# The order of GpSimd's work in an attention step: the projection's subtraction ahead of the head's centring

## The reference

```python
ln_out = _ln(hidden_states, ln_w, ln_b)
q = _fp8_linear_pertensor(ln_out, wq, wq_scale, q_in_scale).reshape(b, s, g, hpg, d)
q = _ln(q, qln_w, qln_b)
k = _fp8_linear_pertensor(ln_out, wk, wk_scale, k_in_scale).reshape(b, s, g, d)
k = _ln(k, kln_w, kln_b)
v = _fp8_linear_pertensor(ln_out, wv, wv_scale, v_in_scale).reshape(b, s, g, d)
core = _gqa(q, k, v).reshape(b, s, nh * d)
...
cat = jnp.concatenate([core, xout], axis=-1)
catq = _div_clamp_fp8(cat, proj_smooth)
return jnp.einsum('bsi,oi->bso', catq, wproj) * (proj_in_scale * proj_w_scale)
```

## Time and profile before

| | us |
|---|---|
| median of 3 runs | 1187.11 |
| lowest and highest | 1186.66, 1187.77 |
| the profiled execution: its time | 1185.83 |
| the profiled execution: its span | 1184.0 |
| TensorE busy | 894.8 (76%) |
| VectorE busy | 957.7 (81%) |
| ScalarE busy | 723.2 (61%) |
| GpSimd busy | 401.2 (34%) |

### The profile page before, as it was taken

The page is one execution under the profiler, slowest core; times in us unless marked ns, Lnnn a source line. Parts: engine busy times, 40 slices in busy tenths (PEclk is TensorE's granted clock), DMA queues, the critical chain, the costliest instruction groups (busy, mean ns, idle before and its releaser), DMA issues. The chain is left out here.

```text
span 1184.0 us, 22559 instructions
## 1 busy us (share of the span) xinstructions
PE 894.8 (76%) x6878; PEld 785.4 (66%) x6878; DVE 957.7 (81%) x2509; ACT 723.2 (61%) x2536; POOL 401.2 (34%) x602
## 2 busy tenths in 40 slices
PE   3620576218878799878879988888899999997638
PEld 3620243217777688767778877777799999996627
DVE  7989898788888899788889877777788888886461
ACT  3442244647777777677777766666777777774313
POOL 0029000003343433344343444444444443433124
PEclk9855598559999999999999999999999999999559
DMA  6030000111001011000101100000000000000400
GB/s 216 1 107 0 0 1 0 36 47 34 2 1 37 2 37 37 2 1 1 37 1 37 46 10 10 10 10 10 10 15 11 15 10 15 11 6 1 147 19 19
DMA packets 24292, 29.97 MB, mean 25 GB/s; under 512 B 1584, under 2 KB 19824, under 8 KB 23920
## 3 DMA queue, kind: packets, MB, share of 16 engines
q1 hardware_dynamic: 23792, 27.51, 7.1%
q0 software_dynamic: 384, 1.05, 0.3%
HBM read 25.93 MB, written 2.62 MB: 24 GB/s over the span
## 5 line engine op out<-in xcount | busy, mean ns | idle before, releaser
L1477 PE MATMUL a_pj_ps<-wp,a_cat 128*128 128x256 f32 x1024 | 157.6, 297 | 91.8 <-POOL a_cat L1231 91.8
L1254 DVE TENSOR_REDUCE a_v<-a_sq 128x6 f32<-128x768 f32 x128 | 121.8, 951 | 116.1 <-ACT a_sq L1407 115.9
L1477 PEld LDWEIGHTS a_pj_ps<-wp,a_cat 128*128 128x128 f32 x1024 | 131.0, 192 | 112.5 <-POOL a_cat L1231 105.9
L1231 POOL TENSOR_TENSOR a_cat<-a_tb,a_mb 128x512 fp32r<-128x512 bf16 x128 | 147.6, 1153 | 63.5 <-DVE a_tb L1293 61.5
L1389 ACT ACTIVATE a_p<-a_kT_sc_ps,a_nmax 128x64 f32<-128x64 f32 x512 | 151.5, 307 | 2.9 <-DVE a_nmax L1261 2.9
L1443 PE MATMUL a_qo_ps<-wq,a_xqf 128*128 128x512 f32 x512 | 151.2, 417 | 0.0
L1218 POOL TENSOR_TENSOR a_pn<-a_p,a_rsum 128x256 f32<-128x256 f32 x128 | 78.8, 616 | 183.8 <-DVE a_rsum L1338 183.8
L1400 ACT ACTIVATE a_sq<-a_kv_ps 128x256 f32<-128x256 f32 x128 | 49.2, 384 | 135.2 <-PE a_kv_ps L1505 66.9
L1535 PE MATMUL a_kT_sc_ps<-a_kT,a_qT 128*128 128x64 f32 x1024 | 128.8, 269 | 0.6 <-ACT a_kT L1403 0.6
L1535 PEld LDWEIGHTS a_kT_sc_ps<-a_kT,a_qT 128*128 128x128 f32 x1024 | 124.3, 192 | 1.2 <-ACT a_qT L1395 1.0
L1389 ACT ACTIVATION_READ_ACCUMULATOR a_p<-a_kT_sc_ps,a_nmax 128x1 f32 x512 | 103.3, 202 | 0.0
(11 more groups left out here) (315 smaller groups left out, 2197.5 us busy)
## 6 DMA issues: line engine op xcount, KB each, us to landing
a_ctx<-in_ctxT SPq DMA_DIRECT2D x32, 128.0 KB, 2.2
w_work<-in_wprojT SPq DMA_DIRECT2D x3, 1024.0 KB, 5.7
x_res<-in_x SPq DMA_DIRECT2D x4, 512.0 KB, 5.4
vT<-in_ctxT SPq DMA_DIRECT2D x2, 1024.0 KB, 9.8
w_work<-in_wqxT SPq DMA_DIRECT2D x2, 1024.0 KB, 5.0
w_work<-in_wkvxT SPq DMA_DIRECT2D x4, 512.0 KB, 4.6
out_x<-x_res SPq DMA_DIRECT2D x4, 512.0 KB, 4.6
tf_work<-in_wqT SPq DMA_DIRECT2D x1, 1024.0 KB, 6.5
```

What stands on the lines that cost most here:

```text
L1231: nc.gpsimd.tensor_tensor(cat[out8.n % 2][:], tb[:], mb[:], ALU.subtract).then_inc(cat_ready, 1)
L1254: norm(nc.vector.tensor_reduce(v6[:], sq[:].rearrange("p (h d) -> p h d", d=D), AX.X, ALU.add))
L1477: last = nc.tensor.matmul(pj_ps[:, pj.turn % 2, :], cat[pj.n % 2][:, a * P:(a + 1) * P], wp[part][:, pj.half * HU + a, :], start=(pj.half ...
```

## The change

GpSimd's subtraction for the projection is issued ahead of the head's two operations instead of behind them, in every step. The conversion stays last. Its waits come with it, and nothing else changes.

```diff
                             rsum[:].unsqueeze(2).broadcast_to([P, 4, S]), ALU.mult).then_inc(pn_ready, 1)
+                    if out8.live:
+                        pool.wait_ge(cadd_ready, out8.count())
+                        wait_unit(pool, pj_done, out8.before(2))
+                        nc.gpsimd.tensor_tensor(cat[out8.n % 2][:], tb[:], mb[:], ALU.subtract).then_inc(cat_ready, 1)
                     head = head_item(u) if u.live else None
                     if head:
                         pool.wait_ge(aw["head_scaled"], head.count)
...
                         nc.gpsimd.tensor_tensor(head.w, head.w, head.sum.broadcast_to([P, D]), ALU.add
                                                 ).then_inc(aw["head_centred"], 1)
-                    if out8.live:
-                        pool.wait_ge(cadd_ready, out8.count())
-                        wait_unit(pool, pj_done, out8.before(2))
-                        nc.gpsimd.tensor_tensor(cat[out8.n % 2][:], tb[:], mb[:], ALU.subtract).then_inc(cat_ready, 1)
                     if u.live and u.half == 0 and u.turn + 1 < N_PHASES * NT:
```

## The result

| | us |
|---|---|
| median of 4 runs, changed kernel | 1089.7 (1088.05 to 1091.3) |
| median of 4 runs, kernel before | 1187.44 (1186.66 to 1189.69) |
| ratio, 95% interval | 0.9174 (0.9152 to 0.9196) |
| the profiled execution: its time, its span | 1091.3, 1089.4 |

The account below looks back on a forecast made before the run. The bound was taken as a closed loop through GpSimd's wait for ScalarE's head scaling. Savings of 27.3, 30.2 and 35.7 us, together 93.2, off 1185.83 give 1092.6, plus 1.28 a median of 1093.9 us; range 1086 to 1110.

Parts of the forecast that it names:

- The bound and the loop: Attention steps with a head: a closed loop through the head's scaling sets 6.78 us; TensorE idles 91.8 us awaiting a_cat.
- step 2: Attention after the change: TensorE's own work, 5.40 us a self and 5.864 a cross step; ScalarE's head scaling hidden.
- step 3: VectorE in self steps with a head: residual and holds put the step at 5.48 us, bounds 5.40 and 5.85.
- step 1: GpSimd's subtraction starts when `tb` is there, ending 1.6 us before TensorE reaches the projection; the 1.32 us wait goes.
- step 5: Cross steps with heads: two falls of TensorE's granted clock, 3.0 us together, taken as gone; bounds 0 and 3.0 us.
- The sum: Attention savings by phase, 27.3, 30.2 and 35.7, together 93.2 us: profiled 1092.6, plus 1.28 gives median 1093.9 us.
- Contention: In self steps, VectorE's small variance is held beside GpSimd's centring: 0.37 us more each, 16 us, total 1110; chance 0.18.
- What would show it: Trace signs: idle ahead of projection under 10 us, self steps 5.4 to 5.5, GpSimd's largest idle still ahead of head.

Follow-up runs that it names:

- the old order without the wait: Kernel before, its order kept (head, subtraction, conversion), but GpSimd takes the head of the step before, already scaled by ScalarE: 1090.25 us, ratio 0.9184.
- `tb` made early: Changed kernel with tb made right behind the normalised query, ahead of residual, normalised key and the weight piece's difference: 1111.88 us, ratio 0.9365.

## Why the prediction was right

- **The bound and the loop.** Right, and shown by the old order without the wait: with the head's wait out of the way, and the head still ahead of the subtraction, the same time comes out. Of the 91.8 us of idle time 3.9 are left.
- **What is late next** (step 2). Right: TensorE's own work is 5.40 and 5.87 us a step, where 5.40 and 5.864 were taken, and ScalarE's logarithm starts 359.29 - 357.44 = 1.85 us behind the square, as in steps without a head.
- **VectorE's part** (step 3). The self step was taken as 5.48 us from steps without a head; it is 5.45, a difference of 1.4 us in all. The stand-in held one thing that head steps don't have: in them the conversion comes behind the centring and misses the variance. Putting it back there gave 5.50 in phase 0. The rest over 5.40 is the residual, as said.
- **The slack** (step 1). The subtraction was to end 1.6 us before TensorE asks for it. It ends 0.51 before (358.97 against 359.48). The working took `tb` from a step of the old pace, 0.7 us ahead of the square; at the new pace VectorE has hardly any idle time, and `tb` is ready at 357.75, 0.31 behind the square. It did not matter here, but doing the subtraction twice shows how near the edge is. A slack read at the old pace has to be redone at the new one.
- **The clock** (step 5). Right that the dips go. The argument against it, that self steps show none, was wrong: the second profile of before has two there, and three in all. So the 3.0 us counted for two dips are those of one execution, not of the kernel.
- **The sum.** 93.2 us were forecast: 27.3, 30.2 and 35.7. Measured were 26.7 + 1.05 = 27.7, 31.1 and 35.5, together 94.3; the spans differ by 94.6. The profiled execution was to take 1092.6 and took 1091.3. The median was to lie 1.28 above the profiled one, as before, and lay 1.6 below it. So of the 4.2 us between the forecast and the median 2.9 come from this offset, which had nothing behind it but the difference seen in the kernel before. The runs of the changed kernel are 1088.05, 1088.27, 1091.13 and 1091.3. Of the two profiled executions the attention's steps take the same time; they differ in where TensorE's clock comes back in the last stage. Windows of the first and of the second profile there:

```profile
1060.00:1075.00 15.00, 15.00 (x66) 12.41 (x65) 0.81 (x3) 10.58 (x16) 9.58 (x8) 0.85 0.00 1
```

```profile
1060.00:1075.00 15.00, 14.86 (x69) 12.23 (x67) 1.21 (x4) 10.57 (x16) 10.14 (x8) 0.90 0.01 2
```

- The second started its projections 1.5 us later (284.70 against 283.25) and yet ends 0.7 us earlier (spans 1088.7 and 1089.4), with the larger share of full clock in this window. That this makes the whole 3 us between the runs is argued, not shown.
- **Contention**, the rival given 0.18, did not come: in the changed kernel's steps with a head, holds of the variance appear only where VectorE is late, and they are 0.17 us or less. Its mechanism is real, though, and it costs 22 us with `tb` made early. A single hold can be larger than the 0.37 us a step assumed: 0.51 on the variance, 0.85 on the difference.
- **What would show it.** One sign was read wrongly ahead: GpSimd's largest idle time is no longer ahead of the head but ahead of the probabilities (L1218, 219.5 us) and of the subtraction.

## What to carry to other kernels

In an engine that runs its queue in order, look at which wait stands ahead of the work that others need; a wait for something side by side with it, here the next phase's weights, costs as if it were the critical work. Steps of the same loop in which that work is absent give the new pace before anything is built, but slacks have to be redone at that pace. When work is moved on GpSimd, look at which VectorE instructions it will then lie beside, and keep away from it those that were held here: a tensor_tensor with two SBUF inputs, and the tensor_scalar instructions.

## What the runs showed of the hardware

- A VectorE instruction with two inputs in SBUF (128x256 f32, 0.42 us) that meets a GpSimd operation of 1.16 us takes 1.27 us and ends 0.29 us behind that operation; a tensor_scalar of 128x6 f32 takes 0.71 us beside a conversion and 1.07 beside a subtraction instead of 0.20, and ends with them; one of 128x512 bf16 takes up to 0.66 us beside the subtraction and 0.29 without it. A multiplication with one input in PSUM (0.42 us) and a reduction of one SBUF input (0.95 us) beside the same subtraction keep their times, and so does the subtraction (1.15 to 1.16 us).
- TensorE's granted clock fell to its lower level, 1.2 GHz, in single steps of the attention in which TensorE idled 1.3 us of 6.8 to 7.3, at a price of 1.5 us each, two and three times an execution and not at the same steps; before the last four steps it did not fall in the seven profiles in which TensorE idled under 0.3 us a step, nor in the one in which it idled 0.8 us a step in phase 0.
